# Attention scores as two full-height products, with part of the low queries made on GpSimd

## What is computed

```python
q = (layernorm(x) @ Wq + bq).reshape(bs, n_ctx, HEADS, d)
kv = (data @ Wkv + bkv).reshape(bs, n_data, HEADS, 2 * d)
k, v = (kv[..., :d], kv[..., d:])
scores = jnp.einsum('bqhd,bkhd->bhqk', q, k) * scale
attn = jax.nn.softmax(scores, axis=-1)
x = x + jnp.einsum('bhqk,bkhd->bqhd', attn, v).reshape(bs, n_ctx, WIDTH) @ Wp + bp
x = x + experts(layernorm(x))        # top 2 of 8, width 256 -> 1024 -> 256
```

## Time and profile before

| what | value |
|---|---|
| median of the runs | 935.6 us (935.13 to 937.54) |
| the profiled execution: its own time | 938.24 us |
| its span, first to last instruction | 936.4 us |
| PE busy | 887.6 us, 95% of the span |
| DVE, ACT, POOL busy | 745.0, 646.3 and 408.9 us |
| scores of block 0 begin | 19.80 us |
| scores of block 31 begin | 293.83 us |
| mean granted TensorE clock | 0.989 of full speed |

### The profile page before, as it was taken

How to read it: one execution, slowest core, us unless ns; L and a number is a source line. 1 busy time by engine, 2 the same in 40 slices (tenths; PEclk the granted TensorE clock), 3 DMA queues, 4 the chain that set the end, 5 groups by cost and what they waited for, 6 DMA issues and landing times.

```text
span 936.4 us, 19131 instructions
## 1 busy us (share of the span) xinstructions
PE 887.6 (95%) x6174; PEld 795.6 (85%) x6174; DVE 745.0 (80%) x1757; ACT 646.3 (69%) x1297; POOL 408.9 (44%) x649
## 2 busy tenths in 40 slices
PE   4999999999998998999999999999999999999995
PEld 3888878887877876788999989899898998998994
DVE  2688888888878888787979788887877877778783
ACT  3676766767666774775977777867776776777773
POOL 3456576777776575330432240605114234052052
PEclk8899999999999999999999999999999999999998
DMA  6332333342255337643756455827817838466442
GB/s 144 66 67 49 74 85 69 86 99 61 63 128 177 114 118 268 182 112 121 217 121 185 135 155 168 240 94 186 278 45 215 282 68 259 177 178 177 147 79 27
DMA packets 132368, 129.17 MB, mean 138 GB/s; under 512 B 59936, under 2 KB 117152, under 8 KB 132128
## 3 DMA queue, kind: packets, MB, share of 16 engines
q1 hardware_dynamic: 119392, 110.36, 38.7%
q0 software_dynamic: 12864, 17.44, 10.3%
HBM read 102.01 MB, written 25.36 MB: 136 GB/s over the span
## 4 chain that ended last, share of the span: by engine, by line
PE 78%; DVE 11%; issue 3%; ACT 3%; another core or an unknown queue 1%; POOL 1%; SPq 1%; DMA 0%; POOLq 0%; DVEq 0%; ACTq 0%
PE bank L1985 35%; PE bank L2029 18%; PE bank L1820 5%; PE bank L1737 4%; PE bank L1977 3%; PE bank L1755 3%; PE bank L1774 2%; DVE maxes L1238 2%; PE bank L1784 2%; PE bank L2017 1%; PE bank L1954 1%; DVE probs L1244 1%; DVE q_l L1279 1%; PE bank L1792 1%
## 5 line engine op out<-in xcount | busy, mean ns | idle before, releaser
L852 POOL DMA_INDIRECT out_rows<-yo,token x68 | 114.4, 1682 | 384.9 <-ACT yo L1095 319.8
L1985 PE MATMUL bank<-xh,wh 128*128 128x512 f32 (+1 forms) x672 | 234.7, 349 | 5.4 <-DVE gate_in L1610 4.8
L1985 PE MATMUL bank<-xl,wh 128*128 128x512 f32 (+1 forms) x672 | 228.9, 341 | 0.0
L1985 PE MATMUL bank<-xh,wl 128*128 128x512 f32 (+1 forms) x672 | 228.5, 340 | 0.0
L1586 DVE TENSOR_TENSOR wl<-raw,wh 128x1024 fp32r<-128x1024 f32 x126 | 152.4, 1220 | 13.0 <-ACT wh L1026 12.1
L1985 PEld LDWEIGHTS bank<-xh,wh 128*128 128x128 f32 x672 | 127.9, 190 | 20.1 <-DVE gate_in L1610 7.5
L2029 PE MATMUL bank<-wh,hh 128*128 128x256 f32 x496 | 141.9, 286 | 1.7 <-issue 1.3
L1985 PEld LDWEIGHTS bank<-xh,wl 128*128 128x128 f32 x672 | 127.8, 190 | 14.9
L2029 PE MATMUL bank<-wh,hl 128*128 128x256 f32 x496 | 140.4, 283 | 0.0
L2029 PE MATMUL bank<-wl,hh 128*128 128x256 f32 x496 | 140.4, 283 | 0.0
L1985 PEld LDWEIGHTS bank<-xl,wh 128*128 128x128 f32 x672 | 128.2, 191 | 10.8
(11 more groups left out here) (195 smaller groups left out, 1861.6 us busy)
## 6 DMA issues: line engine op xcount, KB each, us to landing
raw<-in_W SPq DMA_DIRECT2D x42, 1024.0 KB
raw<-in_Wo SPq DMA_DIRECT2D x25, 1024.0 KB
whole<-in_W SPq DMA_DIRECT2D x8, 1024.0 KB, 7.6
xs<-in_x SPq DMA_DIRECT2D x32, 128.0 KB, 2.7
out_rows<-x SPq DMA_DIRECT2D x32, 128.0 KB, 1.8
shared<-z_rows SPq DMA_DIRECT2D x7, 520.0 KB
bo_row<-in_bo SPq DMA_DIRECT2D x25, 128.0 KB
k_blocks<-k_parts SPq DMA_DIRECT2D x128, 19.2 KB
```

The costliest lines, as they stand in the source:

```text
L852: e.indirect_dma_start(out=out, out_offset=bass.IndirectOffsetOnAxis(ap=token[j % 4][:, s:s + 1], axis=0), in_=yo[j % 2][:, s, :], in_offs ...
L1985: mm = e.matmul(ps[:, h * cols:(h + 1) * cols], ws[split_before(j) % 2][:, w, c, m * P:(m + 1) * P], xx[j % 2][:, c, 0:cols], start=(h == ...
```

## The change

The products of the scores get full height (128 partitions), two for each group instead of three of half height. For that the stationary operand `q_parts` holds, for each group, its high queries in the group's own 64 partitions and its low queries in the other 64. The moving operand of the first product has the group's high keys twice, in both halves, so that it gives (high + low queries) times high keys at once; that of the second has the low keys in the own half and zeros in the other. Around it:

- `k_blocks` gets an axis for the group (twice the size and twice the zeros; buffer 0 lies in the experts' weight buffer, which is free until then), and SyncE's `double_keys(b)` waits for the eight DMAs of `spread_keys(b)` and copies the high blocks to the other half with two more.
- ACT makes the high queries by two activations of 64x512 instead of one of 128x512.
- DVE's `low_queries(b)` makes only the low queries of the batch's first block, by two subtractions of 64x256. Those of the second block (round 2b + 1) are made by POOL, `late_queries(b)`, in POOL's round 2b behind `add_bp(2b)` and ahead of `put_rows`; PE's `scores(2b + 1, 0)` waits for them (`q_late`).
- PE waits for `less_max` (the score bank is free) for each group apart.

```diff
+        q_parts = [sb(f"q_parts{i}", [P, DC, 2, SEQ], F32R) for i in range(2)]
+            def double_keys(b):
+                e.wait_ge(f_kblocks[b % 2], 16 * HPC * (b // 2 + 1))
+                for g in range(2):
+                    own, other = (slice(r * HALF, (r + 1) * HALF) for r in (g, 1 - g))
+                    e.dma_start(k_blocks[b % 2][other, 0, :, g, :, :].bitcast(F32),
+                                k_blocks[b % 2][own, 0, :, g, :, :].bitcast(F32)).then_inc(
+                                    f_kdouble[b % 2], 16)
...
                 if batch and i % 2:
                     load_values(nb)
+                    if nb:
+                        double_keys(nb)
...
                     if nb == 0:
                         spread_keys(nb)
+                        double_keys(nb)
                     store_values(nb)
...
+            def late_queries(b):
+                e.wait_ge(xb_made, 2 * b + 1)
+                put = min(b - 5, LATE_GATES - 2)
+                if put > 0:
+                    e.wait_ge(f_put[(put - 1) % ZR], puts((put - 1) % ZR, put))
+                for g in range(2):
+                    part = slice(g * HALF, (g + 1) * HALF)
+                    other = slice((1 - g) * HALF, (2 - g) * HALF)
+                    e.wait_ge(q_high, 2 * b + g + 1)
+                    e.tensor_tensor(q_parts[b % 2][other, :, g, P:SEQ], q_t[part, :, P:SEQ],
+                                    q_parts[b % 2][part, :, g, P:SEQ].bitcast(F32),
+                                    ALU.subtract).then_inc(q_late, 1)
+                    e.wait_ge(q_late, 2 * b + g + 1)
...
                 if 0 <= i < NT:
                     add_bp(i)
+                if 0 <= i < NT and i % 2 == 0:
+                    late_queries(i // 2)
...
                 if b:
-                    e.wait_ge(q_low, b)
+                    e.wait_ge(q_low, 2 * b)
+                    e.wait_ge(q_late, 2 * b)
...
                 if s == 0 and m == 0:
-                    e.wait_ge(q_low, b + 1)
                     e.wait_ge(f_kblocks[b % 2], 16 * HPC * (b // 2 + 1))
+                    e.wait_ge(f_kdouble[b % 2], 32 * (b // 2 + 1))
+                if s == 1 and m == 0:
+                    e.wait_ge(q_late, 2 * b + 2)
...
-                for k, (qs, w) in enumerate(((q_h, 0), (q_l, 0), (q_h, 1))):
-                    for g in range(2):
-                        mm = e.matmul(
-                            score_bank[(u0 + g) % 3][:, 0:HPB * CTX],
-                            qs[b % 2][g * HALF:(g + 1) * HALF, m, s * P:(s + 1) * P],
-                            k_blocks[b % 2][g * HALF:(g + 1) * HALF, w, m, :, :].rearrange(
-                                "p h k -> p (h k)"), start=(k == 0), stop=(k == 2))
+                for g in range(2):
+                    if s == 0 and m == 0:
+                        e.wait_ge(q_low, 2 * b + g + 1)
+                    if u0 + g >= 3:
+                        e.wait_ge(less_max, u0 + g - 2)
+                    for k in range(2):
+                        mm = e.matmul(score_bank[(u0 + g) % 3][:, 0:HPB * CTX],
+                                      q_parts[b % 2][:, m, g, s * P:(s + 1) * P],
+                                      k_blocks[b % 2][:, k, m, g, :, :].rearrange(
+                                          "p h k -> p (h k)"),
+                                      start=(k == 0), stop=(k == 1))
```

More of the change, by code:

```diff
@@ L274, in build @@
         f_x, f_ctx = sems("f_x", XR), sems("f_ctx", 2)
-        f_kblocks, f_vstore, f_vload = (sems(n, 2) for n in ("f_kblocks", "f_vstore", "f_vload"))
+        f_kblocks, f_kdouble, f_vstore, f_vload = (
+            sems(n, 2) for n in ("f_kblocks", "f_kdouble", "f_vstore", "f_vload"))
         f_x1, f_put = sems("f_x1_", 3), sems("f_put", ZR)
@@ L288, in build @@
                              "xf_summed", "xf_var", "z_made", "rstd_step", "rstd_made"))
-        (k_low, q_low, v_added, v_spread, max_found, less_max, recip_made, attn_made, best_made,
+        (k_low, q_low, q_late, v_added, v_spread, max_found, less_max, recip_made, attn_made, best_made,
          best_index) = (
-            sem(n) for n in ("k_low", "q_low", "v_added", "v_spread", "max_found", "less_max",
+            sem(n) for n in ("k_low", "q_low", "q_late", "v_added", "v_spread", "max_found", "less_max",
                              "recip_made", "attn_made", "best_made", "best_index"))
@@ L373, in build @@
         v_rep = [sb(f"v_rep{i}", [P, KB, VW]) for i in range(2)]
-        k_blocks = [sb(f"k_blocks{i}", [P, 2, DC, HPB, CTX], F32R) for i in range(2)]
-        q_h = [sb(f"q_h{i}", [P, DC, SEQ], F32R) for i in range(2)]
-        q_l = [sb(f"q_l{i}", [P, DC, SEQ], F32R) for i in range(2)]
+        k_blocks = [first_parts[:, 2, :, :, :].rearrange("p w c n -> p (w c n)")[
+            :, 0:4 * DC * HPB * CTX].rearrange("p (w m g h k) -> p w m g h k", w=2, m=DC, g=2, h=HPB),
+                    sb("k_blocks1", [P, 2, DC, 2, HPB, CTX], F32R)]
+        q_parts = [sb(f"q_parts{i}", [P, DC, 2, SEQ], F32R) for i in range(2)]
         v_blocks = [sb(f"v_blocks{i}", [P, KB, BLOCK_HEADS, VW]) for i in range(2)]
@@ L931, in queries @@
                     e.wait_ge(scores_mm, SCORES_OF_BATCH * (b - 1))
-                e.activation(q_h[b % 2][:, :, :], q_t[:, :, :], ACTF.Copy).then_inc(q_high, 1)
+                for g in range(2):
+                    part = slice(g * HALF, (g + 1) * HALF)
+                    e.activation(q_parts[b % 2][part, :, g, :], q_t[part, :, :],
+                                 ACTF.Copy).then_inc(q_high, 1)
             def exp_scores(i, m):
@@ L1277, in low_queries @@
             def low_queries(b):
-                e.wait_ge(q_high, b + 1)
-                e.tensor_tensor(q_l[b % 2][:, :, :], q_t[:, :, :],
-                                q_h[b % 2][:, :, :].bitcast(F32), ALU.subtract).then_inc(q_low, 1)
+                for g in range(2):
+                    part = slice(g * HALF, (g + 1) * HALF)
+                    other = slice((1 - g) * HALF, (2 - g) * HALF)
+                    e.wait_ge(q_high, 2 * b + g + 1)
+                    e.tensor_tensor(q_parts[b % 2][other, :, g, 0:P], q_t[part, :, 0:P],
+                                    q_parts[b % 2][part, :, g, 0:P].bitcast(F32),
+                                    ALU.subtract).then_inc(q_low, 1)
             def x1_sums(i):
```

19 lines of the change are left out of this document (9 added, 10 removed).

## The result

The changed kernel takes **1023.03 us** (median of 4 runs, 1021.5 to 1026.73), against 936.57 us of the kernel before beside it (4 runs, 935.13 to 942.63): ratio **1.092**, 95% interval [1.086, 1.097]. The forecast was 1005 us in a range of 968 to 1032, so sign and range held, and the time is 18 us above it.

The account below looks back on a forecast made before the run. PE was taken as the bound, with DVE close; 938.2 + 10.2 (beginning) + 35 (ring, products' saving included) - 1 (end of round 31), less 2.6 for the median, gave 980, plus 25 (clock) 1005 us; range 968 to 1032.

Parts of the forecast that it names:

- The ring: Attention: odd-block scores on PE wait for POOL, POOL for DVE, DVE for PE; +35 us over 15 batches.
- the lower bound: POOL's two 64x256 subtractions: half the partitions take half the time, 0.37 us each.
- The clock: PE's idle gaps ahead of odd-block scores bring the 1.2 GHz level, losing 1.7 us a batch, 25 us.
- Rival 1: Attention: the wait for POOL's queries costs its time, but PE's clock stays up; 980 us, chance 0.25.
- The beginning: Start of the kernel: two extra key-copy DMAs and POOL's later work delay the scores of block 1; +10.2 us.
- The products: Scores on PE: four full-height products save 0.21 us a call, 13.4 us over 64 calls if PE stays the bound.
- Rival 4: Scores on PE: half-height products were worth three slots, four cost more; 10 us more, 1015 us, chance 0.05.
- Rivals 2 and 3: POOL in time: only the products count, 925 us (0.05); or second key copies make PE wait, 940 us (0.03).

Follow-up runs that it names:

- e3: The kernel before, half-height products and single keys kept, with only POOL's late queries in round 2b and PE's wait for them added; 1021.0 us, ratio 1.086.
- e9: The changed kernel with 28 full-height products of 308 columns on PE ahead of its wait for the late queries; 993.0 us, ratio 1.063.
- e4: The changed kernel with 50 small bf16 products of 128 columns on PE ahead of its wait for the late queries; 1026.4 us, ratio 1.091.
- e8: e2 with the keys of two batches made a round earlier, so SyncE spreads and copies them earlier; 934.5 us, ratio 1.001.
- e6: e2 without the second key copies and PE's wait for them, one product left out of the result; 929.5 us, ratio 0.994.
- e1: The changed kernel with all low queries made on DVE and no wait for POOL; 978.0 us, ratio 1.038.
- e2: The changed kernel with POOL's low queries made a round earlier, behind the bias of round 2b - 1; 973.1 us, ratio 1.034.

## Why the prediction was right, and where its sum was short

**The ring** was the right mechanism, and its place and nearly its size too. `e3` shows that it alone is enough, `e9` gives its length at full clock. Against my steps from T, the start of the odd block's scores (T = 221.58 in the rows of `e9`):

| step | forecast | measured in `e9` |
|---|---|---|
| DVE's second softmax | T + 4.5 | 226.03 = T + 4.45 |
| reciprocals | T + 8.3 | 230.07 = T + 8.49 |
| last statistics | 8.07 later | 238.15, 8.08 later |
| bias done | 2.46 later | 240.63, 2.48 later |
| two subtractions and PE | 1.6 later | 242.42, 1.79 later |
| sum | 20.4 | 20.84 |

The reciprocals came behind DVE's leg, not PE's: the scores of block 20 began at T + 8.26 (229.84), and DVE had no idle row between its second softmax and the reciprocals. The subtractions cost what I took them at: 32 of them, 0.719 to 0.725 us each in the changed kernel. So 64x256 takes GpSimd as long as 128x256 (0.73), and the lower bound (half of it) fell.

**What was short in the ring** is the mean: I took 20.2 because every second batch has no low keys, and it was 20.91. The batch from T = 221.58 is just one without low keys, and DVE still needed 8.08 us from the reciprocals to the statistics. The 0.39 us saved there were used up by small operations that got longer: the cast of `pick` takes 0.58 us in the changed kernel (at 229.41), where it took 0.27 before (at 210.24). No run tested the cause, but the trace of the changed kernel shows when it happens: the 11 casts of `pick` that run beside POOL's `v_blocks` take 0.54 to 0.68 us, the other five 0.17 to 0.33. In `e9` the batches without low keys take 20.8 us where my steps give 20.0, and those with them 21.0 where they give 20.4; two long last batches (21.9 and 22.5) and a short early one (18.3) about cancel. Together 0.7 us a batch, 10 us.

**The clock** was the right second term, 25 us forecast and 31 measured (22.98 - 20.91 = 2.07 a batch instead of 1.7). The step that was short is its length. I took 3.4 us at the low level from the one row behind 363.32; only three of the 15 waits have that, the mean is 6.1 us, 4.8 of it with PE at work again. Of these 4.8 us a little less than half is lost (2.07), so "half of it" nearly held. It is lost on the ring's leg on PE: up to DVE's second softmax it takes 224.04 - 217.50 = 6.54 us there against 4.45 at full clock. Blocks 17 and 19 don't fit so well: with 3.4 us at the low level their batches are still 2.3 and 2.4 us longer than in `e9`. That the record misses part of the low level there, as in the second half of `e4`, would fit; no row shows it. Rival 1 (the clock stays up, 980) is out: `e9` had to be built to see its kernel, and it gave 993.

**The beginning** was forecast at +10.2 us and is +11.5. The copies cost more than 2.7: block 0 began at 23.91, 4.1 us later.

**The products** save nearly what I forecast, though the ring hides it in the changed kernel's time. By ends, in the chain of the work that ended last, before and then `e8`:

```profile
108.94 0.63 PE bank L1737 x6
109.57 0.37 PE bank L1792 x2
109.94 0.22 PE bank L1861 x2
110.16 0.44 PE bank L1755 x4
```

```profile
112.55 0.62 PE bank L1794 x4
113.17 0.22 PE bank L1848 x2
113.38 0.22 PE bank L1917 x2
113.60 0.44 PE bank L1811 x4
```

From the scores to the transposed probabilities it was 1.22 us and is 1.05: 0.17 for the first call of a round. PE's starts say nearly the same over rounds 6 to 27, where no wait falls into the call. From the start of the operation ahead of a call to the start of the one behind its transposes it was 1.32 us (median of 22 calls) and is 1.16 in `e6`, 0.16 less; for the second call of a round 1.20 us (13 calls) and 1.00, 0.20 less. The mean is 0.18 and not 0.21, so 0.72 us a batch, and that is just what `e6` shows between blocks 7 and 21.

Where the gain lies is less clear. In a second call the three parts (operation ahead to first product, to the transposes, to what follows them) take 0.31, 0.62 and 0.28 us before and 0.03, 0.76 and 0.22 in `e6`; in a first call 0.20, 0.63 and 0.49, and 0.08, 0.65 and 0.44. So the four full-height products are not cheaper by themselves, and the gain stands at the two edges of the half-height group. That is what a cost of the switch would look like; no run separates it from another cause at the same place. Rival 4 is out: the call is cheaper as a whole. My step "the saving is 13.4 us if PE stays the bound" has the condition that fails: in `e8` 0.47 of the 0.72 us arrives, because DVE's softmax makes PE wait.

**The rivals that were mis-priced.** Rivals 2 and 3 say what happens when POOL is in time. I gave 925 us (0.05) more than 940 (0.03). `e1` and `e2` give 978 and 973: the key copies are a real wait, and they cost not 1 us a batch but (973.1 - 929.5) / 15 = 2.9, the beginning included, or 2.5 by the ratios (1.034 and 0.994). Two numbers of the step were off. The slack that I read as about a third of a batch is a quarter: in the kernel before the last spreading issue ended at 204.03 and the scores of block 22 began at 208.22, 4.2 us. And what follows the last issue is not two landings of 1.4 us and 1.3 of issue, 4.1, but the 5.84 of `e2`, since other DMAs stand between them on the queue (until 217.12), and from the last issue of the copies, 154 KB each, to PE it is 2.57 us and not 1.4. With a wait of 2 us comes the clock again (0.961 over the span in `e2`, 0.988 in `e6`). In the ring the copies are hidden, as said: the scores at 228.01, the first of an even block, have no wait.

**The excess of 19 us** over the forecast for the profiled execution (1026.7 - 1007.4) is thus the ring's mean length (10), the clock (6), the beginning (1) and the end of round 31, which was to be 1 us quicker and is not (from block 31 to the end 643.0 us for 642.6).

## What to carry to other kernels

Before work moves to an idler engine, look at what that engine itself waits for there, and follow it back: if the chain comes from the waiting engine, the move closes a ring, and its whole length is the new time of the loop. Here two small subtractions in the wrong round cost 82 us by themselves (`e3`, 1021.0 against 938.8), and a round earlier `e8` with them is at the time of the kernel before. Remove the first wait on paper and price the next one by its worst instance, not by its mean slack: behind this ring stood a DMA that follows a DMA, worth another 40 us. And a product form that saves 0.18 us a call is worth only what the engine next in line lets through: in `e8`, with both waits gone, the kernel is where it was. And don't read an average as one effect: `e4` looked like nothing and was a gain in one half and a loss in the other.

## What the runs showed of the hardware

- Six half-height products (64x308, in pairs) between full-height operations take as a group 0.16 us (first calls) and 0.20 us (second calls) more than four full-height ones, from the start of the operation ahead to the start of the one behind the transposes (medians, `before` and `e6`). The extra time stands at the group's edges: 0.31 us ahead of the first product for 0.03, and 0.28 for 0.22 over the transposes behind, in second calls.
- PE's rows and its clock can be off by 2 us in 7 where the rows of the engines that read its results agree with each other: in `e4` the granted clock reads 1.00 from 206 to 214 us, and PE's `queries` start 4.6 us ahead of ACT's copy of them. The Trainium skill warns of the clock's record (TensorE: Matmul & The Clock Gate, Part 1: recorded clock events were seen to be unreliable) and of the ends of PE's rows (Perfetto Trace Analysis, Tensor Engine Instruction: they are estimated). Here the start of the engine that reads the result is the better witness.
- The granted clock falls while PE still waits: in 14 of the 15 waits of 2.8 to 4.1 us the low level begins 0.4 to 2.6 us before the scores do, and it lasts 6.8 us at 12 of them and 3.4 us at three. Behind the start of the scores that leaves 4.8 us, of which 2.07 are lost.
- A filler in the wait can give this back, but not surely: 28 matmuls of 308 columns, 4.25 us, with no wait left, did it in every batch; 50 of 128 columns, 2.95 us, with 0.9 to 1.3 us left, did it just as well up to block 11 and not from block 13 on. These two differ in format, width, data and cover, and none of them changes within `e4`.
- Issuing a DMA on ACT takes 0.68 us, as on SyncE (0.66), and ACT's next operation waits for the last of them: it starts at 18.31, right behind the eight issues that end at 18.27.
- A cast of 128x4 on DVE takes 0.17 us at the shortest, and 0.54 to 0.68 beside POOL's `v_blocks` in the changed kernel.
